# Router logits with the weight columns stationary and the tokens moving

## The reference, cut to what matters

```python
x = x + _L0_gnn_ref(xn, ...) + _L0_mix_ref(xn[None], ...)[0]
x = x + _L0_ffn_ref(_layernorm(x)[None], ...)[0]

def _L0_ffn_ref(x, Wr, br, ...):
    xt = x.reshape(N, D)                      # D = 256
    logits = xt @ Wr + br                     # Wr: 256 x 8, the router
    probs = jax.nn.softmax(logits, axis=-1)
    top_p, top_idx = jax.lax.top_k(probs, 2)
    weights = top_p / top_p.sum(axis=-1, keepdims=True)
    ...                                       # each token through its two experts
```

## Time and profile before

| | us |
|---|---|
| median of three runs | 2523.36 |
| lowest and highest run | 2522.85, 2523.72 |
| the profiled execution, its time | 2523.16 |
| its span, first to last instruction | 2521.3 |
| busy: PE, DVE, ACT, POOL | 2209.7, 1289.2, 1173.2, 1489.7 |

### The profile page before, as it was taken

How to read it: one execution, slowest core, us unless ns; L and a number is a source line. 1 busy time by engine, 2 the same in 40 slices (tenths; PEclk the granted TensorE clock), 3 DMA queues, 4 the chain that set the end, 5 groups by cost and what they waited for, 6 DMA issues and landing times.

```text
span 2521.3 us, 52177 instructions
## 1 busy us (share of the span) xinstructions
PE 2209.7 (88%) x12141; PEld 1789.7 (71%) x12142; DVE 1289.2 (51%) x2312; ACT 1173.2 (47%) x2845; POOL 1489.7 (59%) x1493
## 2 busy tenths in 40 slices
PE   0999996689999899999999986858999999999995
PEld 0677775566666666666666664736999999999995
DVE  8799998566565666656666564452222222222221
ACT  2444442566666666666666664552223323323321
POOL 6766656577777777777777775002445444444542
PEclk9999997799999999999999999557999999999998
DMA  4000002433333333333333359266666566666564
GB/s 144 1 1 1 1 1 76 120 105 105 105 104 106 104 105 105 104 106 104 105 105 104 104 115 83 87 216 203 177 186 182 173 186 185 175 181 187 177 177 137
DMA packets 140354, 299.21 MB, mean 119 GB/s; under 512 B 31650, under 2 KB 81140, under 8 KB 140055
## 3 DMA queue, kind: packets, MB, share of 16 engines
q0 software_dynamic: 72672, 143.45, 23.2%
q1 hardware_dynamic: 67639, 155.29, 19.1%
HBM read 264.21 MB, written 40.84 MB: 121 GB/s over the span
## 4 chain that ended last, share of the span: by engine, by line
PE 62%; DVE 12%; DVEq 9%; issue 7%; POOL 5%; DMA 3%; ACT 0%; SPq 0%; POOLq 0%; ACTq 0%
PE B L1330 20%; PE B L1423 15%; PE B L1432 14%; DVE ACC L538 5%; DVEq L656 3%; POOL BIG L493 3%; DVE BIG L651 3%; DMA BIG<-table,W2A 2%; DVEq L786 2%; PE B L1303 2%; PE B L1392 1%; DVEq L778 1%; PE B L1370 1%; PE B L1235 1%; PE B L1268 1%
## 5 line engine op out<-in xcount | busy, mean ns | idle before, releaser
L493 POOL DMA_INDIRECT BIG<-table,W2A x880 | 832.1, 946 | 290.6 <-issue 231.2
L538 DVE TENSOR_TENSOR ACC<-ACC,B 128x512 f32 x880 | 605.3, 688 | 429.4 <-PE B L1330 323.0
L1330 PE MATMUL B<-BIG,W2A 128*128 128x256 f32 x1760 | 437.8, 390 | 82.5 <-DVE ACC L538 55.3
L1033 ACT ACTIVATE BIG<-B,SMALL 128x128 f32<-128x128 f32 (+1 forms) x889 | 250.4, 387 | 524.4 <-PE B L1423 524.4
L1330 PE MATMUL B<-BIG 128*128 128x256 f32 x1760 | 430.6, 389 | 48.2 <-DVE ACC L538 18.5
L1330 PEld LDWEIGHTS B<-BIG,W2A 128*128 128x128 f32 x1760 | 301.9, 189 | 195.0 <-issue 168.6
L1330 PEld LDWEIGHTS B<-BIG 128*128 128x128 f32 x1760 | 308.2, 190 | 162.4 <-issue 119.8
L1423 PEld LDWEIGHTS B<-BIG,W1A 128*128 128x128 f32 x3360 | 394.3, 193 | 7.9 <-DVE BIG L541 2.6
L1423 PE MATMUL B<-BIG,W1A 128*128 128x128 f32 x3360 | 395.0, 276 | 2.0 <-DVE BIG L541 2.0
L1432 PE MATMUL B<-W2A,BIG 128*128 x1680 | 380.2, 379 | 0.7 <-DVE BIG L538 0.7
L513 POOL DMA_INDIRECT sums<-BIG,SMALL x105 | 170.6, 1625 | 335.9 <-DMA sums<-BIG,SMALL 290.4
(11 more groups left out here) (218 smaller groups left out, 2182.0 us busy)
## 6 DMA issues: line engine op xcount, KB each, us to landing
W1A<-in_w SPq DMA_DIRECT2D x105, 1024.0 KB, 5.1
BIG<-table,W2A POOLq DMA_INDIRECT x880
W2A<-in_w SPq DMA_DIRECT2D x1, 8192.0 KB, 31.3
sums<-ACC SPq DMA_DIRECT2D x1, 6400.0 KB, 22.9
table<-ACC SPq DMA_DIRECT2D x7, 896.0 KB, 7.1
out_dram<-sums SPq DMA_DIRECT2D x1, 6250.0 KB, 22.2
W2A<-in_x SPq DMA_DIRECT2D x1, 6144.0 KB
token_x<-BIG SPq DMA_DIRECT2D x24, 256.0 KB, 2.1
```

The source lines that it names most:

```text
L493: pool.indirect_dma_start(G[h][:, u, :], None, table, bass.IndirectOffsetOnAxis(ap=dst_T[:, c:c + 1], axis=0)).then_inc(gath[h][u // 2], 16)
L538: return dve.tensor_tensor(o, a, b, op)
L1033: return nc.scalar.activation(o, i, fn, **kw)
L1330: last = mm(B[u][:, k * D:(k + 1) * D], OH[h % 2][:, u, k * P:(k + 1) * P], G[h][:, u, :], start=True, stop=True)
```

## The change

The router's operands change places. `wr_s[:, k, :]` (128 features x 8 experts) is stationary, and the 256 tokens of a pair, a strided view of x2T, move: two products a pair, accumulated over k, into 8 partitions of bank `B[5 + j % 2]`. ACT copies this 8x256 result into SBUF (`logits_T`, two buffers), and PE transposes it tile by tile, 8x128 to 128x8, into the columns of `B[4]` where the logits stood before. Two semaphores are new, logitT_ps and logitT_ready. ACT's wait for the x2T buffer is now on logitT_ps; a product waits for the copy of two pairs before, a copy for the small transposes of two pairs before. In ACT's list the copy of pair j-2 stands behind transposed_x2 of pair j-1; in PE's list the small transposes of pair j-1 stand behind the products of pair j.

```diff
+        logits_T = [W1A[0:E, R0 + 8 * NE + D * k:R0 + 8 * NE + D * (k + 1)] for k in range(2)]
+        logitT_ps, logitT_ready = sem("logitT_ps"), sem("logitT_ready")
...
                 act.wait_ge(x2T_ps, j + 1)
                 if j >= 4:
-                    act.wait_ge(logit_ps, 2 * (j - 4) + 2)
+                    act.wait_ge(logitT_ps, j - 3)
                 cp(x2T[j % 4][:, 0:n * KD, :], B[j % 4][:, 0:n * D].rearrange("p (g n) -> p g n", n=P)).then_inc(x2T_ready, 1)
+
+            def transposed_logits(j):
+
+                n = min(2, NT - 2 * j)
+                act.wait_ge(logitT_ps, j + 1)
+                if j >= 2:
+                    act.wait_ge(logit_ps, 2 * (j - 2) + 2)
+                cp(logits_T[j % 2][:, 0:n * P], B[5 + j % 2][0:E, 0:n * P]).then_inc(logitT_ready, 1)
...
                     if t % 2 == 1 and t >= 3:
                         transposed_x2(t // 2 - 1)
+                        if t >= 5:
+                            transposed_logits(t // 2 - 2)
...
             transposed_x2(NPAIR - 2)
+            transposed_logits(NPAIR - 3)
             transposed_x2(NPAIR - 1)
+            transposed_logits(NPAIR - 2)
+            transposed_logits(NPAIR - 1)
...
             def router_product(j):
+                n = min(2, NT - 2 * j)
                 pe.wait_ge(x2T_ready, j + 1)
+                if j >= 2:
+                    pe.wait_ge(logitT_ready, j - 1)
+                for k in range(KD):
+                    last = mm(B[5 + j % 2][0:E, 0:n * P], wr_s[:, k, :], x2T[j % 4][:, k:n * KD:KD, :],
+                              start=k == 0, stop=k == KD - 1)
+                last.then_inc(logitT_ps, 1)
+
+            def token_logits(j):
+                pe.wait_ge(logitT_ready, j + 1)
                 for t in range(2 * j, min(2 * j + 2, NT)):
-                    for k in range(KD):
-                        last = mm(B[4][:, t * E:(t + 1) * E], x2T[j % 4][:, t % 2 * KD + k, :], wr_s[:, k, :],
-                                  start=k == 0, stop=k == KD - 1)
-                    last.then_inc(logit_ps, 1)
+                    nc.tensor.transpose(B[4][:, t * E:(t + 1) * E], logits_T[j % 2][:, t % 2 * P:(t % 2 + 1) * P], ident[0:E, 0:E]
+                                        ).then_inc(logit_ps, 1)
 
             transpose_x2(0)
             for j in range(NPAIR):
                 if j + 1 < NPAIR:
                     transpose_x2(j + 1)
                 router_product(j)
+                if j > 0:
+                    token_logits(j - 1)
+            token_logits(NPAIR - 1)
```

## The result

The changed kernel takes 2511.05 us (median of six runs, 2509.12 to 2512.38) against 2523.54 us for the kernel before beside it (2521.35 to 2525.56): a ratio of 0.995, 95% interval 0.9938 to 0.9962, 12.5 us less. The forecast was 10.6 us more. The span of the profiled execution is 2508.1 us, 13.2 us less than before.

A forecast was written before the change was run, and what follows sets the result against it. The router stage was taken as bound by PE's weight loads at half clock. Pairs +9.9 us, tail +1.1 and slot_experts' wait -0.4 gave +10.6 us, so 2534.0 us, range 2513 to 2539.

The forecast's parts named there:

- What bounds the kernel: Router stage: PE alone, bound by weight loads at half clock, 2.461 us a pair; changes there reach the end.
- the transfer that I had named: Behind the logits: slot_experts' store lands close to W2A's 8 MB load; DVE's 0.47 us wait may go, -0.4 us.
- The sum at the half clock: Router stage at 1.2 GHz: 2.93 us a pair against 2.46, over 21 pairs +9.9 us (8.0 to 12.0).
- The clock: Router stage: PE stays at 0.50 under the new mix of transposes and products; forecast B, 2534.0 us, chance 0.70.
- Rival A: Router stage: more moving columns lift the clock, ACT bounds at about 1.8 us a pair; 2512 to 2515 us, chance 0.17.
- Two slow pairs before the rise: Router stage, within the faster case: two pairs pass at half clock before the clock rises, each losing 0.47 us.
- The late slot_experts: Behind the logits, within the faster case: W2A's load starts closer to them, slot_experts up to 2.9 us late.
- ACT's order: ACT in the router stage: the extra copy's wait for its product hides, with some 1.5 us to spare.
- Tail: Router stage's end, last big transposes to DVE: 4.09 us instead of 2.99, +1.1 us (0.6 to 1.6).

The follow-up runs named there:

- the run with both sets of products: Kernel before, with the change's two wide products added per pair as unused extra work: 2523.78 us against 2523.35, ratio 0.9999.
- the last chain above: Waits in the changed kernel with W2A's load issued behind the first four W1 loads, second timing: 2511.47 us against 2527.04.

## Why the prediction was wrong

**What bounds the kernel: right.** The stage was PE's alone and its end passes on one to one, but for the transfer that I had named: 14.8 us at the logits, 12.7 behind the wait for slot_experts. What I called bound by weight loads hung on the clock as well: L1370's eight records took 1.51 us at 0.50 and 0.79 at 1.00.

**The sum at the half clock: right in sign, somewhat low.** Transposes 0.95 us (0.95) and wide products 1.80 (1.70) were measured in the slow pairs of the run with both sets of products. The two small transposes took 0.31 us (0.38) in the one pair at 0.50 that the last chain above shows; 0.38, two L1370 records, was my lower bound, and it did not hold. At 1.00 they cost 0.21 us. Added up from these runs, a pair at 0.50 comes to 3.06 us, against 2.93 in the forecast and 2.46 before: 21 of them would have lost 12.6 us instead of 9.9.

**The clock: wrong, and it alone set the sign.** The failing step is the paragraph "Where I chose: the clock". Its argument was that nothing in the trace had risen under such a mix, because the blocks of products stand between transposes and have 8 output rows. Both reasons fell on the chip: a block of transposes alone lifted the clock, and so did products with 8 stationary columns alone. In place of 21 slow periods that lose 9.9 us the runs showed a clock of 1.00 through the steady part and 21 periods of 1.764 us, 14.65 us less than before. The Trainium skill, "TensorE: Matmul & The Clock Gate", "Part 4: PE-mode transpose", on which I had leaned, says that the full clock doesn't engage for transposes. Its timings there are for bf16. The float32 run with transposes alone differs from it (0.50 to 1.00, spacing 0.22 to 0.11 us), and the measurement decides. The reading of the trace that misled me was the router stage before: it is full of transposes and stays at 0.50. Transposes are not what kept it there, since alone they raise the clock. With the old eight records between them it stayed at 0.50, and when lifted by hand it was lost again: at about 1599 and 1612 in one run, at 1634 in another. What it is about these records, which load 128 columns in order to move 8, no run separates; a block of them alone was not run. L1392's products, also at 0.50, are a second such case, equally untested.

**Rival A: right in kind and nearly in size.** It gave 2512 to 2515 us. Its terms: a period of about 1.8 us (1.76), of which PE's own was put at 1.52. PE needs 1.76: the wide products cost 0.96 instead of 0.86 and the four transposes 0.59 instead of 0.44. ACT's share, put at about 1.8, came out at 1.72, so PE sets the period and not ACT, by 0.04 us. Two slow pairs before the rise: none in this execution, since the rise came before the steady part. The late slot_experts: up to 2.9 us, measured 2.1 more than before. The chance, 0.17, was the mistake, not the price.

**ACT's order: right.** The copy of pair j-2 makes nobody late: 0.4 us of waiting for products in 35 us of the stage. **Tail:** 2.75 us; the 4.09 us were for the half clock.

## What to carry to other kernels

Where PE reads as fully busy at half clock, take the clock itself as a term of the time. Here a stage that read as 100% busy needed 2.46 us of PE a pair at 0.50 and 1.28 at 1.00, and work that raised the clock cost nothing in the total. Ask of each change whether the new mix raises the clock from below, not only whether it would hold it; try it with a block of the new instruction in an idle gap, one kernel for each kind of instruction. And before the sign of a forecast is left to a clock, give its other level the chance that an untested rule deserves.

## What the runs showed of the hardware

- Float32 transposes raised PE's clock without any product: 0.50 at 1585.37, when the block began, and 1.00 from about 1591. Products with 8 stationary columns did the same: begun at 1585.04, 1.00 from about 1590.6.
- Strictly more work on PE in this stage left the total where it was (ratio 0.9999): 2.44 us a pair with both sets of products at 1.00, 2.46 with one at 0.50.
- One bf16 product of 512 columns a pair held the clock at 1.00 from about 1602 to 1639 in a mix that otherwise lost it within about 10 us. It had not kept the lift before that one, and in another run it never raised the clock again from 0.50.
- The length of a wait of PE did not decide over the clock: 1.00 outlasted waits of 2.22 and 2.45 us in two executions of the changed kernel, and fell at the end of one of 1.86 us with W2A's load moved.
- A store of 0.5 KB from 128 partitions took 7.4 to 7.9 us to land in the four runs with no large load ahead of it. In the ten with W2A's load ahead it took 7.4 to 11.4 us and landed 0.1 to 1.1 us behind that load.
